# Later loans of one bank, two scores moved into a wait, and the last batch's queries in neighbouring steps

## The reference, cut to what matters

```
x += tanh(g)  * attention_A(norm(x), ctx)            1 head of 256, mask added, 512 x 1601 scores
x += tanh(g') * attention_B(norm(x))                 4 of 16 heads chosen by a router, head size 64
x += tanh(g)  * attention_C(norm(x), ctx)            16 heads of 16, 512 x 1601 scores each
x += tanh(g') * expert(norm(x))                      1 of 8 experts per token, 256 -> 1024 -> 256
```

## Time and profile before

| what | us |
|---|---|
| median of 3 runs (lowest, highest) | 2777.71 (2775.05, 2779.29) |
| profiled execution, its own time | 2776.35 |
| its span | 2774.5 |
| TensorE busy | 2617.1 (94%) |
| VectorE busy | 1721.6 (62%) |
| ScalarE busy | 1447.8 (52%) |
| GpSimd busy | 280.3 (10%) |

### The profile page before, as it was taken

One profiled execution on the slowest core, in us unless ns is written; L12 is line 12 of the kernel. 1 busy time (PEld: TensorE's weight loads), 2 busy tenths in 40 slices (PEclk: granted clock), 3 DMA queues, 4 the chain that ended last, 5 costly groups with the idle time before them and its releaser, 6 DMA issues.

```text
span 2774.5 us, 39396 instructions
## 1 busy us (share of the span) xinstructions
PE 2617.1 (94%) x13626; PEld 1276.9 (46%) x13626; DVE 1721.6 (62%) x4190; ACT 1447.8 (52%) x2939; POOL 280.3 (10%) x341
## 2 busy tenths in 40 slices
PE   8989999999999999999999999999999989999998
PEld 4543434443334433443445333443345323349997
DVE  3557776567666776577666775777656778853111
ACT  2423565457454656457555655466545746663232
POOL 1200200020001100020002000110002000012221
PEclk9999999999999999999999999999999999999999
DMA  5611412241232313241324223241323122169994
GB/s 211 167 59 47 120 42 91 58 128 28 83 91 63 91 42 112 55 121 37 103 51 111 52 59 103 63 104 42 112 53 89 19 54 74 34 231 373 372 362 165
DMA packets 215526, 296.37 MB, mean 107 GB/s; under 512 B 50534, under 2 KB 181326, under 8 KB 215319
## 3 DMA queue, kind: packets, MB, share of 16 engines
q1 hardware_dynamic: 198428, 222.87, 28.8%
q0 software_dynamic: 16080, 70.16, 7.4%
q10 hardware_dynamic: 816, 0.79, 0.1%
HBM read 232.87 MB, written 60.50 MB: 106 GB/s over the span
## 4 chain that ended last, share of the span: by engine, by line
PE 78%; DVE 9%; ACT 6%; issue 4%; SPq 2%; DMA 1%; POOL 0%; ACTq 0%; POOLq 0%; DVEq 0%
PE PS L1695 12%; PE PS L1647 10%; PE PS L1678 10%; DVE mxC L2256 7%; PE PS L1320 7%; PE PS L1288 6%; PE PS L1830 5%; PE PS L1840 5%; PE PS L1518 2%; PE PS L1415 2%; PE PS L1349 2%; PE PS L1438 2%; ACT reg L1175 2%; PE PS L1306 2%; PE PS L1430 2%
## 5 line engine op out<-in xcount | busy, mean ns | idle before, releaser
L1175 ACT ACTIVATE reg<-PS 128x512 f32<-128x512 f32 (+1 forms) x1664 | 963.0, 599 | 928.0 <-PE PS L1678 922.3
L2256 DVE TENSOR_REDUCE mxC<-PS 128x1 f32<-128x400 f32 (+1 forms) x2048 | 1090.6, 570 | 508.1 <-PE PS L1647 490.7
L1647 PE MATMUL PS<-reg 96*128 96x400 bf16 (+1 forms) x2048 | 663.4, 337 | 44.5 <-DVE mxC L2256 17.5
L1678 PE MATMUL PS<-reg 99*128 99x512 bf16 (+1 forms) x1664 | 606.4, 384 | 20.3 <-ACT reg L1175 18.4
L1695 PE MATMUL PS<-reg 128*17 128x512 f32 (+1 forms) x3328 | 439.5, 600 | 1.1 <-DVE reg L2280 0.7
L1647 PEld LDWEIGHTS PS<-reg 96*128 96x128 bf16 x2048 | 194.3, 98 | 521.1 <-DVE mxC L2256 382.6
L1678 PEld LDWEIGHTS PS<-reg 99*128 99x128 bf16 (+1 forms) x1664 | 163.9, 100 | 346.1 <-ACT reg L1175 193.9
L1288 PE MATMUL PS<-reg 128*128 128x512 f32 (+1 forms) x512 | 204.4, 515 | 14.3 <-DVE small L2005 13.4
L1320 PE MATMUL PS<-reg 128*128 128x512 f32 (+1 forms) x416 | 211.1, 600 | 0.8 <-ACT reg L1038 0.8
L1214 ACT ACTIVATE reg<-PS,reg 128x128 f32<-128x128 f32 x312 | 89.2, 369 | 197.6 <-PE PS L1830 197.6
L1830 PEld LDWEIGHTS PS<-reg 128*128 128x128 f32 x1248 | 145.0, 192 | 2.7 <-issue 0.8
(11 more groups left out here) (269 smaller groups left out, 2493.7 us busy)
## 6 DMA issues: line engine op xcount, KB each, us to landing
reg<-in_D_W SPq DMA_DIRECT2D x78, 1024.0 KB, 8.5
reg<-in_A_mask POOLq DMA_DIRECT2D x30, 800.5 KB, 7.2
dramK<-reg SPq DMA_DIRECT2D x144, 100.0 KB
dramV<-reg SPq DMA_DIRECT2D x48, 272.0 KB, 3.1
reg<-in_ctxT POOLq DMA_DIRECT2D x8, 1601.0 KB, 10.0
reg<-in_ctx POOLq DMA_DIRECT2D x8, 1536.0 KB, 7.6
reg<-dramQ SPq DMA_DIRECT2D x32, 384.0 KB, 5.7
dramQ<-reg SPq DMA_DIRECT2D x90, 128.0 KB
```

The costliest lines, as they stand in the source:

```text
L1175: act.activation(pr[u % RING][0:r, :], PS[0:r, S_PLAN[NU * b + u][0], :], ACT.Exp).then_inc(a_expC, 1)
L1647: last = mm(PS[:, bank, 0:w], qs[(NG * bb + g) % 3][0:ROWS, h, t * P:(t + 1) * P], ks[g % 2][0:ROWS, h, c0:c0 + w], start=True, stop=True)
L1678: last = mm(PS[0:r, bank, :], ks[g % 2][0:STK, h, c * P:c * P + r], qs[(NG * b + g) % 3][0:STK, h, :], start=True, stop=not with_mask)
L2256: v.tensor_reduce(mxC[:, h, t, j:j + 1], PS[:, M_PLAN[bb, g, i][0], 0:M_CH[j][1]], AX.X, ALU.max).then_inc(v_mx, 1)
```

## The change

It moves entries of the tables and gives two bank functions a case for the last batch. No operation is added or removed.

1. **SPARE.** The second stretch in which F2 is lent begins at step 132 and no longer at 131, the third at 149 and no longer at 147. Chunks 32 to 34 and 61 to 63 of the group ahead therefore use the two MB banks.
2. **SECOND.** Scores 2 and 3 of batch 1's A are issued at step 151 and no longer at 164 and 166, with their masks at step 160 (the new table M; elsewhere M is one step behind S). All that follows in batch 1's A stands four steps earlier, and so does the end of the opening (W_END, W_PIECE, W_ROWS).
3. **LAST.** For the last batch XC stands at steps 143 and 144 (143 and 146 before), in banks F2 and F0; QC at 145 and 146 (149 and 151 before), in F1 and F0. PIECES_LATE, which spreads the first group's chunks of that batch, begins at step 5 of the group and not at 8, with 12122 in place of 1222.

```
-PIECES_LATE = "0" * 8 + "1222" * 9 + "10000000"
+PIECES_LATE = "0" * 5 + "12122" * 8 + "0000000"
...
+def plan(n):
+    return LAST if n == B - 1 else LOOP
...
+LAST = LOOP._replace(XC=(143, 144), QC=(145, 146))
...
+U_S1 = [145, 148, 151, 151, 164, 166, 168, 169] + [174 + 8 * t + d for t in range(2) for d in range(4)]
 SECOND = FIRST._replace(LA=100, XA=(112, 115), QG=(139, 142),
-                        S=[145, 148, 164, 166] + [170 + 8 * t + d for t in range(3) for d in range(4)],
-                        T=[174 + 8 * t + d for t in range(3) for d in range(4)] + [198, 200, 202, 204],
+                        S=U_S1, M=[146, 149, 160, 160] + [u + 1 for u in U_S1[4:]],
+                        T=[170 + 8 * t + d for t in range(3) for d in range(4)] + [194, 196, 198, 200],
...
-W_BRANCH, W_PIECE, W_ROWS = 152, (194, 226), 231
-W_END = 237
-
-SPARE = ((U_RL + 2, U_XA[0]), (U_PVB[1] + 3, U_XC[0]), (U_XC[1] + 1, NU))
+W_BRANCH, W_PIECE, W_ROWS = 152, (190, 222), 227
+W_END = 233
+
+SPARE = ((U_RL + 2, U_XA[0]), (U_PVB[1] + 4, U_XC[0]), (U_XC[1] + 3, NU))
...
 def x_bank(L, k):
+    if L == norm_c(B - 1):
+        return (F2, F0)[k]
     return (F2, F1)[k] if L in (norm_a(0), norm_b(0), norm_c(0)) else F2
...
 def q_bank(n, m):
-    return F1 if n else (F0, F1)[m]
+    return (F1, F0)[m] if n == B - 1 else F1 if n else (F0, F1)[m]
...
-                elif m:
+                elif m and n < B - 1:
                     pe.wait_ge(v_tq, 2 * n + 1)
...
-                    prepare(b + 1, u, LOOP, piece)
+                    prepare(b + 1, u, plan(b + 1), piece)
...
-                    if u == p.S[i] + 1:
+                    if u == p.M[i]:
                         add_mask(m, i)
```

More of the change, by code:

```diff
@@ L81 @@
 N_LO = 6
-Plan = namedtuple("Plan", "SC OA LB XB RL K V QB KB VB LA XA SB TB PVB OB LC QG XC QC S T PV wrap ctx")
+def plan(n):
+    return LAST if n == B - 1 else LOOP
+Plan = namedtuple("Plan", "SC OA LB XB RL K V QB KB VB LA XA SB TB PVB OB LC QG XC QC S M T PV wrap ctx")
 LOOP = Plan(SC=12, OA=U_OA, LB=U_LB, XB=U_XB, RL=U_RL, K=U_K, V=U_V, QB=U_QB, KB=U_KB, VB=U_VB, LA=U_LA, XA=U_XA,
-            SB=U_SB, TB=U_TB, PVB=U_PVB, OB=U_OB, LC=U_LC, QG=U_QG, XC=U_XC, QC=U_QC, S=U_S, T=U_T, PV=U_PV,
-            wrap=NU, ctx=170)
+            SB=U_SB, TB=U_TB, PVB=U_PVB, OB=U_OB, LC=U_LC, QG=U_QG, XC=U_XC, QC=U_QC, S=U_S, M=[u + 1 for u in U_S], T=U_T,
+            PV=U_PV, wrap=NU, ctx=170)
+LAST = LOOP._replace(XC=(143, 144), QC=(145, 146))
 O_SB = [111 + 3 * k + 3 * (k >= 4) for k in range(8)]
+U_S0 = [14, 15, 16, 17, 18, 19, 20, 21, 26, 27, 28, 29, 34, 35, 36, 37]
 FIRST = Plan(SC=49, OA=(75, 77), LB=79, XB=(86, 88), RL=92, K=[85, 87, 94, 96, 98, 99, 100, 101],
@@ L91 @@
              OB=(150, 151), LC=153, QG=(10, 12), XC=(161, 163), QC=(165, 167),
-             S=[14, 15, 16, 17, 18, 19, 20, 21, 26, 27, 28, 29, 34, 35, 36, 37],
+             S=U_S0, M=[u + 1 for u in U_S0],
              T=[22, 23, 24, 25, 30, 31, 32, 33, 38, 39, 40, 41, 43, 44, 45, 46],
              PV=[48 + c for c in range(2 * CT)], wrap=0, ctx=0)
+U_S1 = [145, 148, 151, 151, 164, 166, 168, 169] + [174 + 8 * t + d for t in range(2) for d in range(4)]
 SECOND = FIRST._replace(LA=100, XA=(112, 115), QG=(139, 142),
-                        S=[145, 148, 164, 166] + [170 + 8 * t + d for t in range(3) for d in range(4)],
-                        T=[174 + 8 * t + d for t in range(3) for d in range(4)] + [198, 200, 202, 204],
-                        PV=[206 + c * 20 // 18 for c in range(18)] + [226, 227, 228, 229] + [232, 233, 234, 235], ctx=77)
+                        S=U_S1, M=[146, 149, 160, 160] + [u + 1 for u in U_S1[4:]],
+                        T=[170 + 8 * t + d for t in range(3) for d in range(4)] + [194, 196, 198, 200],
+                        PV=[202 + c * 20 // 18 for c in range(18)] + [222, 223, 224, 225] + [228, 229, 230, 231], ctx=77)
 U_RAMP, U_MARK, U_RANK, U_SUM, U_TAB, U_SLOT = 2, 41, 46, (60, 75, 90, 112, 126, 140), (156, 157), (158, 159, 160, 161)
 U_TJ, U_ONE, U_IDS, U_WL = (162, 163, 164, 165, 166), (167, 168, 169, 170, 171, 172, 173), 190, (157, 158, 159)
-W_BRANCH, W_PIECE, W_ROWS = 152, (194, 226), 231
-W_END = 237
-SPARE = ((U_RL + 2, U_XA[0]), (U_PVB[1] + 3, U_XC[0]), (U_XC[1] + 1, NU))
+W_BRANCH, W_PIECE, W_ROWS = 152, (190, 222), 227
+W_END = 233
+SPARE = ((U_RL + 2, U_XA[0]), (U_PVB[1] + 4, U_XC[0]), (U_XC[1] + 3, NU))
 class Ticks:
@@ L720, in fill @@
                 if n < B:
-                    bring(n, u, LOOP)
+                    bring(n, u, plan(n))
             def bring(n, u, p):
@@ L994, in _ @@
                     if b + 1 < B:
-                        prepare(b + 1, u, LOOP)
+                        prepare(b + 1, u, plan(b + 1))
                     if b + 2 < B:
```

## The result

Five executions of each kernel: before 2776.61 us (2775.05 to 2779.29), after 2762.05 us (2757.7 to 2768.3). The ratio is 0.9946, 95% interval 0.9936 to 0.9957: 15.0 us faster (11.9 to 17.8). Forecast were 15.5 us and 2761.5.

What follows compares the result with a forecast made beforehand. TensorE, busy 94% of 2774.5 us, was taken as the bound, so only its waits could pay. Loans 8.4 + opening 0.7 + last batch 6.4 = 15.5 us, giving 2761.5 us; range for 8 in 10: 2756 to 2769.

Steps and rivals of the forecast that it cites:

- Loans: At steps 131 and 147 of six middle batches, chunks no longer wait for copies: 0.55 and 0.85 us each, 8.4 in all.
- Rival 2: Loans give nothing because two banks pace the chunks by VectorE; total gain 7 us, 2769.5; chance 8%.
- Opening: Two scores go into TensorE's 7.40 us wait for normed rows; 2.1 us shrink to 0.7 gained, bounds -1.5 and 2.1.
- T4: Turn of chunk 4 in the opening, after the second exponential; to start at about 180.35 and no longer at 181.04.
- ScalarE's issues: Six DMA issues in the opening, now ahead of the second exponential; three cost 3.02 us, the other three 2.05.
- The mishap carried for the branch: In the opening, the branch's fetch might use all of the 7.40 us wait; then 2.1 us lost, not 0.7 gained.
- Last batch: Batch 6, preparing batch 7: maxima start 5.7 us earlier and their phase gains 0.7; 6.4 us, bounds 1 and 9.
- The stop at M: Ahead of the transposes of the maxima's row in the last batch, TensorE has a new stop of 4.6 us.
- Rival 1: Last batch gives about 1 us: new stop, slow clock until the maxima, row behind stores; total gain 10, 2766.5; chance 20%.
- Rival 3: Clock stays high in the last batch and opening issues overlap: 9 + 2.1 + 8.4 = 19.5 us, 2757; chance 12%.
- Rival 4: TensorE at 1.2 GHz after the new stop through the last batch's whole maxima phase; 18 us slower, 2796; chance 3%.
- The row of maxima behind the stores: Last batch: the 12 KB row, needed at step 156, queues behind six stores; just in time, any store delay stops TensorE.

Runs made afterwards that it cites:

- e3_last: The kernel before with the last batch's part of the change alone: 2776.93 us, ratio 0.9994.
- e11: The changed kernel with 28 dummy transposes ahead of the last batch's row of maxima, none in the opening: 2757.12 us, ratio 0.9929.
- e4: The changed kernel with dummy transposes in both stops, 36 in the opening and 28 ahead of the last batch's row of maxima: 2757.95 us, ratio 0.9932.
- e5: e3_last with 28 dummy transposes ahead of the transposes of the maxima's row: 2770.48 us, ratio 0.9978.
- e8: The changed kernel with 42 dummy transposes in the opening, 28 in the last batch, whose second query projection stands a step later: 2758.97 us, ratio 0.9934.
- e12: The changed kernel with 36 dummy transposes in the opening, 16 in the last batch, whose second query projection stands a step later: 2761.74 us, ratio 0.9938.
- e10: The changed kernel with 36 dummy transposes in the opening's stop alone: 2763.68 us, ratio 0.9951.
- e6: The kernel before with 54 dummy transposes in the opening's stop and nothing else changed: 2781.42 us, ratio 1.0015.

## Why the prediction was right, point by point

**Loans (8.4 forecast): right in size and in cause.** 1.4 to 1.6 us per middle batch against 1.40, a wait of 0.40 at step 147 as worked out, nothing given back. Alone they gave 8.9 in seven. Rival 2 falls.

**Opening (0.7 forecast, bounds -1.5 and 2.1): 2.8 measured (0.3 to 5.3), by another path.** The median lies above the bounds, the interval reaches into them; net of its head start T4 came 0.63 and 2.07 us earlier in the two profiles of after, 0.88 in that of the part alone. The mis-sized term is ScalarE's issues: six took 4.18 us and not the 5.07 of the earlier trace rows, those after the first group 0.6 each, and the copies of PSUM ran between them. So T4 followed T0 by 7.05 us and not 8.45. In the first profile of after T4 still started at 180.41 on the clock of the earlier trace rows, as forecast (180.35), since T0 had come at 173.36 there and not at 171.9: two errors that cancelled, which is luck. In the second one T0 came at 171.91, as forecast, and the second exponential ended at 178.77, 1.5 us before the 180.3 forecast. What delayed T0 in the first is the clock, which took part of the 2.1 us. (With the idle time at T0 these make 3.2, and not the 3.4 of the working; nothing rests on it.) From the rows' transposes to T0 it was 14.69 us before, 14.06 and 12.62 in the two profiles of after, and 11.16 with the stop filled. In before 2.9 us of work were done at 1.2 GHz there, in the first profile of after 5.9, in the second 3.1. The working left this out: it shortened the stop and let the clock come back when it had. The mishap carried for the branch could have been ruled out from the trace of before: its line shows that the branch ended at 154.3 and so took 2.4 of the 7.40 us of the stop, and not all. In after it ended 4.2 us before the stop did.

**Last batch (6.4 forecast, bounds 1 and 9): right at the full clock, not at the low one.** 6.3 in the profile of e3_last, 6.1 at the median with the stop filled, but 0.8 in the profile of after (under the lower bound), 5.1 in its second one, 1.7 at the median of the part alone. By steps: the wait for ScalarE's copy was 0.86 (0.95 forecast). The stop at M was 3.5 and not 4.6: M came when it should, and TensorE arrived later, 0.47 of it a wait for an exponential in front of step 150. The stores' first issue to the load took 7.0 and not 5.5 to 6, and the load 3.5 to 3.9 and not 4 to 5 (5.2 in e11): the two about cancel. M to the first maximum took 8.3 to 8.7 filled in e4, e5 and e8 (8.3 forecast), and up to 12.5 unfilled. The phase took 32.0 to 32.4 in most profiles (33.4 forecast), 32.7 in e12 and 33.6 in e11. The clock's bound was 3.5 us; it took 4.

**Rival 1** (the last batch gives nothing) was given 20%, with the mechanism that came true: it is what the profiled execution of after shows in batch 6, and 3 executions in 11 took its time or a little more (2767.1 to 2768.3, its 2766.5). In the one that was profiled batch 6 accounts for 4.3 of the 9.6 us beside the second profile, so that the total is not rival 1's alone. What was not forecast is that forecast and rival are no alternatives for the kernel, but for each execution of it. The median is the forecast's, as most executions aren't hit that hard.

That the total came within half a microsecond (15.0 for 15.5) is partly luck. By medians of the parts alone, the opening gave 2 us more than forecast and the last batch 4 us less, with intervals of 2.5 us to either side.

**Rival 3** (clock high, 2757): approached by eight executions from 2757.7 on, and by the filled kernels. **Rival 4** (slower) didn't come: the longest low stretch lasted 13.7 us, from 0.5 us ahead of M on, and not the 31 more it needed.

**The row of maxima behind the stores:** the trace of after shows no wait for it, at the low clock; at the full one TensorE waits 0.4 us in e4_busy and 1.55 in e12_split_short. The prediction feared this order for the rings. What the traces show lies ahead of them: SyncE issues in order, the six stores keep it for 3.7 us, and the row is issued 0.05 us after the sixth. M came 1.2 us earlier in e12 than in e8, and the wait grew by 1.1 us, from 0.43.

## What to carry to other kernels

Where a shared buffer is lent, ask at each loan whether the ordinary buffers are free sooner. Waiting for a busy engine's copy seven times cost more than having a buffer less.

A stop that is removed may come back elsewhere, shorter, and then cost more than its length, as TensorE works at half speed behind it. Judge such a change by many executions and by their clocks, and try what a filled stop gives before believing in the new order.

Fill a stop only where its length and what interrupts it are known: the same filler gave some 4 us in one place, and cost as much in another. And look for the wait that then ends last: here it was a load, which no filler brings forward.

## What the runs showed of the hardware

Behind the unfilled stop of 3.5 us TensorE was at 1.2 GHz in all five profiles that have it, for 3.4 to 13.7 us; the cause of this spread is open. In before, without the stop, it was at the full clock behind M until 2264.8. Low stretches also came where no long stop was near (2324.5 in after), so part of each kernel's spread is not explained here.

Three DMA issues on ScalarE took 2.39 or 3.02 us in a row, and 0.59 to 0.60 each in the second group of the new order. Six on SyncE took 3.7 us.

TensorE's one branch is recorded for 6.0 to 7.2 us in the six kernels with the old opening, and for 4.5 to 4.7 us in the eight where it comes some 2 us later, behind two more scores; SyncE's one in before took 0.04 us. Behind it, pauses of 0.82, 2.23 and 2.76 us without a releaser came between equal, independent matmuls in three of the five openings with fillers (e10, e12, e6) and none in e4 and e8.
